# Edge sums of a graph network: sixteen edge tiles share one stretch of PSUM columns, with columns read as 5-bit steps

## The reference

```python
h = jnp.maximum(_layernorm(x), 0.0)
agg_src  = segment_sum(h[src], dst, 6250)
agg_edge = segment_sum(edge_attr_128, dst, 6250)
x = x + relu(concatenate([h, agg_src, agg_edge], 1) @ W.T + b)

h = jnp.maximum(_layernorm(x), 0.0)
h = relu(mean_agg(h) @ W1_l + b1 + h @ W1_r)     # mean over h[src] of the edges into each node
x = x + relu(mean_agg(h) @ W2_l + b2 + h @ W2_r)
```

## Time and profile before

| | |
|---|---|
| device time, 3 runs | 2033.34 us median (2031.09 to 2033.35) |
| profiled execution | span 1450.0 us from the first to the last instruction; its own device time is not recorded |
| build stage | about 117 to 665 us of the span |
| busy share of the span | PE 94%, PEld 85%, DVE 56%, POOL 45%, ACT 34% |

### The profile page before, as it was taken

One profiled execution on the slowest core, in us unless ns is written; L12 is line 12 of the kernel. 1 busy time (PEld: TensorE's weight loads), 2 busy tenths in 40 slices (PEclk: granted clock), 3 DMA queues, 4 the chain that ended last, 5 costly groups with the idle time before them and its releaser, 6 DMA issues.

```text
span 1450.0 us, 34753 instructions
## 1 busy us (share of the span) xinstructions
PE 1368.8 (94%) x12165; PEld 1235.0 (85%) x12166; DVE 812.4 (56%) x1837; ACT 490.1 (34%) x1389; POOL 654.9 (45%) x772
## 2 busy tenths in 40 slices
PE   3777999999999999998999999999999999999996
PEld 3656999999999899997888888888888888888885
DVE  8686898888888888882454545432222222221221
ACT  2632123455688888882333232311111110000000
POOL 5400000011121121215777777167777745777775
PEclk9988999999999999999999999999999999999998
DMA  6108778888999988886565556566666665666663
GB/s 182 29 2 221 202 221 230 242 248 237 261 271 266 273 260 260 262 269 222 161 214 177 175 199 162 193 195 196 205 196 207 187 194 190 220 210 214 213 203 74
DMA packets 284762, 295.12 MB, mean 204 GB/s; under 512 B 19461, under 2 KB 250064, under 8 KB 284672
## 3 DMA queue, kind: packets, MB, share of 16 engines
q1 hardware_dynamic: 233861, 212.90, 46.9%
q0 software_dynamic: 26016, 69.24, 16.9%
q10 hardware_dynamic: 24795, 11.74, 2.8%
HBM read 245.70 MB, written 48.11 MB: 203 GB/s over the span
## 4 chain that ended last, share of the span: by engine, by line
PE 84%; POOL 2%; issue 2%; DMA 2%; ACT 2%; DVE 0%; ACTq 0%; POOLq 0%; DVEq 0%; SPq 0%
PE edge_banks L1065 41%; PE edge_banks L1023 20%; PE banks L997 10%; PE edge_banks L1096 4%; PE edge_banks L1019 4%; PE banks L1083 3%; POOL shared L833 2%; ACT shared L1252 1%; DMA shared<-in_edge_attr 1%; PE edge_banks L1072 1%; PE banks L1077 1%; ACT banks L1247 0%; DMA shared<-g_rows,list_src 0%; DMA shared<-counts 0%; ACT shared L1229 0%
## 5 line engine op out<-in xcount | busy, mean ns | idle before, releaser
L833 POOL DMA_INDIRECT shared<-g_rows,list_src x555 | 541.9, 976 | 230.8 <-issue 167.2
L1065 PE MATMUL edge_banks<-g_even,shared 128*128 128x257 f16 (+1 forms) x3822 | 444.7, 273 | 4.4 <-DMA shared<-counts 4.4
L1065 PEld LDWEIGHTS edge_banks<-g_even,shared 128*128 128x128 fp8e3 x3822 | 372.4, 97 | 62.6 <-issue 4.6
L1023 PE MATMUL edge_banks<-shared 128*128 128x128 f32 x2744 | 345.3, 277 | 4.4 <-issue 4.0
L1023 PEld LDWEIGHTS edge_banks<-shared 128*128 128x128 f32 x2744 | 325.8, 193 | 7.6 <-issue 7.0
L812 POOL DMA_DIRECT2D counts<-shared x156 | 76.4, 490 | 487.8 <-ACT shared L1252 472.8
L1639 DVE SCALAR_TENSOR_TENSOR shared<-edge_banks,shared,own 128x128 f32<-128x128 f32 x98 | 34.3, 350 | 367.6 <-PE edge_banks L1065 339.4
L1065 PE MATMUL edge_banks<-shared 128*128 128x256 f16 x1911 | 225.8, 272 | 0.2 <-DVE own L1621 0.2
L1551 DVE TENSOR_TENSOR shared<-iota,shared 128x3528 f16<-128x3528 f16 x98 | 195.5, 1995 | 51.2 <-PE banks L997 50.8
L1252 ACT ACTIVATE shared<-banks 128x392 uint16<-128x392 f32 x312 | 152.2, 488 | 184.6 <-PE banks L997 174.2
L1065 PEld LDWEIGHTS edge_banks<-shared 128*128 128x128 fp8e3 x1911 | 185.3, 97 | 30.7 <-DVE own L1621 0.5
(11 more groups left out here) (278 smaller groups left out, 997.6 us busy)
## 6 DMA issues: line engine op xcount, KB each, us to landing
shared<-in_edge_attr SPq DMA_DIRECT2D x195, 512.0 KB, 4.5
shared<-counts SPq DMA_DIRECT2D x117, 784.0 KB, 5.2
counts<-shared POOLq DMA_DIRECT2D x156, 196.0 KB, 3.8
shared<-g_rows,list_src POOLq DMA_INDIRECT x555
shared<-hot_rows SPq DMA_DIRECT2D x20, 304.0 KB, 2.9
g_rows<-g_even SPq DMA_DIRECT2D x1, 3136.0 KB, 15.5
g_rows<-shared ACTq DMA_DIRECT2D x49, 64.0 KB
g_rows<-g_even ACTq DMA_DIRECT2D x49, 64.0 KB
```

The lines of the kernel that those rows point to most:

```text
L833: pool.indirect_dma_start(ring_g[use % RING][:, t, 0:2 * D], None, g_rows[r], bass.IndirectOffsetOnAxis(ap=list_src[:, at:at + 1], axis=0) ...
L1023: mm = pe.matmul(edge_wide[bank][:, :, at], ring[:, bank * GROUP_TILES + j, :], hot_dst[u][:, k, (j - 1) * SPREAD:j * SPREAD].unsqueeze(1) ...
L1065: mm = pe.matmul(acc[s][:, 0:wide], stream8[slot][:, order[h], :], G[r % 2][:, order[h], 0:wide], start=h == 0, stop=h == BLOCKS - 1, skip ...
```

## The change

The two groups of an iteration now share one stretch of 170 columns in one bank, so that there is one clearing product of 170 columns per iteration instead of two of 128, and one addition of 170 columns into `edge_t` instead of two of 128. The one-hots are 24 columns wide instead of 32, and written three times instead of four (3 x 170 = 510 of the bank's 512 columns). Offsets are counted from the start of the iteration's stretch. A group's four offsets no longer fit into three fields of 128; they are packed as one start and three steps of 5 bits, so the sequencer shifts, masks and adds them up. For k=1 all four offsets are needed, for k=0 three. DVE waits once, not twice, for `edge_free` in an iteration, and in a loop's pass a wait for `hot_ready` stands ahead of `hot_a`; the numbers that PE waits for on `edge_free` are halved.

```diff
-REACH = 32
-SPREAD = 32
-COPIES = 4
-EDGE_COLS = 128
-COL_UNIT = 128
+REACH = 24
+SPREAD = 24
+COPIES = 3
+EDGE_COLS = 170
+STEP_BITS = 5
...
-        edge_ps = [flat[i][:, 0:EDGE_COLS] for i in range(4)]
-        edge_wide = [f.rearrange("p (k c) -> p k c", c=EDGE_COLS) for f in flat]
+        edge_ps = [flat[i][:, 0:EDGE_COLS] for i in range(2)]
+        edge_wide = [flat[i][:, 0:COPIES * EDGE_COLS].rearrange("p (k c) -> p k c", c=EDGE_COLS) for i in range(2)]
...
                                     if n == HALF - 1:
-                                        pe.wait_ge(S["edge_free"], i * 2 + 3)
+                                        pe.wait_ge(S["edge_free"], i + 2)
...
                         def edges(k, packed, load_next):
-                            bank = 2 * u + k
-                            low, middle, high, rest = col_regs[u][k]
-                            pe.reg_alu(rest, packed, COL_UNIT, ALU.python_divide)
-                            pe.reg_alu(low, rest, -COL_UNIT, ALU.mult)
-                            pe.reg_alu(low, low, packed, ALU.add)
-                            pe.reg_alu(high, rest, COL_UNIT, ALU.python_divide)
-                            pe.reg_alu(middle, high, -COL_UNIT, ALU.mult)
-                            pe.reg_alu(middle, middle, rest, ALU.add)
-                            col = [0] + [pe.snap(g, donate=True, min_val=0, max_val=EDGE_COLS - SPREAD) for g in (low, middle, high)]
-                            for c in col[1:]:
-                                pe.lower_val((c + bank * 512) * 4 + (PSUM_BASE + BANKS * 2048) if bank else c * 4 + (PSUM_BASE + BANKS * 2048))
-                            pe.wait_ge(batch_landed[bank], it * 16 + 16)
-                            pe.matmul(edge_ps[bank], ring[:, bank * GROUP_TILES, :], hot_dst[u][:, k, FIRST_HOT:GROUP_HOT],
-                                      start=True, stop=True, skip_group_check=True)
-                            for j in range(1, GROUP_TILES):
-                                at = slice(0, SPREAD) if j < PAIR else bass.ds(col[j // PAIR], SPREAD)
-                                mm = pe.matmul(edge_wide[bank][:, :, at], ring[:, bank * GROUP_TILES + j, :],
-                                               hot_dst[u][:, k, (j - 1) * SPREAD:j * SPREAD].unsqueeze(1).broadcast_to([P, COPIES, SPREAD]),
+                            batch = 2 * u + k
+                            col = col_regs[u][k]
+                            step = step_regs[u][k]
+                            pe.reg_alu(col[0], packed, 3 * STEP_BITS, ALU.logical_shift_right)
+                            for q in range(1, 4):
+                                pe.reg_alu(step, packed, (3 - q) * STEP_BITS, ALU.logical_shift_right)
+                                pe.reg_alu(step, step, (1 << STEP_BITS) - 1, ALU.bitwise_and)
+                                pe.reg_alu(col[q], col[q - 1], step, ALU.add)
+                            moved = [pe.snap(g, donate=True, min_val=0, max_val=EDGE_COLS - SPREAD) for g in col]
+                            for c in moved[1 - k:]:
+                                pe.lower_val((c + u * 512) * 4 + (PSUM_BASE + BANKS * 2048) if u else c * 4 + (PSUM_BASE + BANKS * 2048))
+                            pe.wait_ge(batch_landed[batch], it * 16 + 16)
+                            for j in range(GROUP_TILES):
+                                tile = ring[:, batch * GROUP_TILES + j, :]
+                                if k == 0 and j == 0:
+                                    pe.matmul(edge_ps[u], tile, hot_dst[u][:, FIRST_HOT:WINDOW_HOT], start=True, stop=True, skip_group_check=True)
+                                    continue
+                                at = slice(0, SPREAD) if k == 0 and j < PAIR else bass.ds(moved[j // PAIR], SPREAD)
+                                n = k * GROUP_TILES + j - 1
+                                mm = pe.matmul(edge_wide[u][:, :, at], tile,
+                                               hot_dst[u][:, n * SPREAD:(n + 1) * SPREAD].unsqueeze(1).broadcast_to([P, COPIES, SPREAD]),
                                                start=False, stop=True, skip_group_check=True)
...
                     dve.tensor_tensor(hot_b, iota_b, along(b_tab, LO_B), ALU.is_equal).then_inc(S["b_ready"], 1)
+                    if not first:
+                        dve.wait_ge(S["hot_ready"], it * 2)
                     dve.tensor_tensor(hot_a, iota_a, along(a_tab, LO_A), ALU.is_equal)
...
-                        for k in range(2):
-                            dve.wait_ge(S["edge_free"], i * 2 + (k + 1))
-                            add_edges(bass.ds(at[2 * u + k], EDGE_COLS), 2 * u + k)
+                        dve.wait_ge(S["edge_free"], i + 1)
+                        add_edges(bass.ds(at[u], EDGE_COLS), u)
```

More of the change, by code:

```diff
@@ L169, in message_passing @@
         hot_bv = place(6264, LO_B * STEPS_ROW // 2).bitcast(F16).rearrange("p (l s) -> p l s", s=STEPS_ROW)
-        GROUP_HOT = GROUP_TILES * SPREAD + EDGE_COLS - SPREAD
-        FIRST_HOT = (GROUP_TILES - 1) * SPREAD
-        hot_dst = [place(6408 + i * 2 * GROUP_HOT, 2 * GROUP_HOT).rearrange("p (k c) -> p k c", c=GROUP_HOT) for i in range(2)]
-        assert 6408 + 4 * GROUP_HOT <= 8500
+        WINDOW_HOT = TILES_IT * SPREAD + EDGE_COLS - SPREAD
+        FIRST_HOT = (TILES_IT - 1) * SPREAD
+        hot_dst = [place(6408 + i * WINDOW_HOT, WINDOW_HOT) for i in range(2)]
+        assert 6408 + 2 * WINDOW_HOT <= 8500 and COPIES * EDGE_COLS <= 512 and REACH <= 1 << STEP_BITS
         ring = place(8500, 4096).rearrange("p (j c) -> p j c", c=D)
@@ L982, in build @@
                 col_regs = [[registers(pe, 4, f"col{u}_{k}_") for k in range(2)] for u in range(2)]
+                step_regs = [registers(pe, 2, f"step{u}_") for u in range(2)]
                 pe.wait_ge(S["words_taken"], WORDS)
@@ L1383, in _ @@
             dve.tensor_scalar(in_dense, w8_i[0:HOLDERS, 0:PER], float(DENSE * WINB), None, ALU.is_lt)
-            link(dve.tensor_scalar(col_pack, ident[:, 3 * PAIR::GROUP_TILES], float(COL_UNIT), None, ALU.mult))
-            link(dve.tensor_tensor(col_pack, col_pack, ident[:, 2 * PAIR::GROUP_TILES], ALU.add))
-            link(dve.tensor_scalar(col_pack, col_pack, float(COL_UNIT), None, ALU.mult))
-            dve.tensor_tensor(col_pack, col_pack, ident[:, PAIR::GROUP_TILES], ALU.add)
+            of_pair = [ident[:, q * PAIR::GROUP_TILES] for q in range(4)]
+            unit = float(1 << STEP_BITS)
+            link(dve.scalar_tensor_tensor(out=col_pack, in0=of_pair[0], scalar=unit, in1=of_pair[1], op0=ALU.mult, op1=ALU.add))
+            link(dve.scalar_tensor_tensor(out=col_pack, in0=col_pack, scalar=unit, in1=of_pair[2], op0=ALU.mult, op1=ALU.add))
+            dve.scalar_tensor_tensor(out=col_pack, in0=col_pack, scalar=unit - 1.0, in1=of_pair[3], op0=ALU.mult, op1=ALU.add)
             dve.wait_ge(S["base_up"], 2)
@@ L1531, in build, with add_edges @@
                 dve.wait_ge(S["zeroed"], 2 * BANKS)
-                def add_edges(at, bank):
-                    dve.tensor_tensor(edge_t[:, at], edge_t[:, at], edge_ps[bank], ALU.add).then_inc(S["edge_free"], 1)
+                def add_edges(at, u):
+                    dve.tensor_tensor(edge_t[:, at], edge_t[:, at], edge_ps[u], ALU.add).then_inc(S["edge_free"], 1)
                 def body(it, first):
@@ L1573, in build @@
                     body(it, False)
-                last = registers(dve, 4, "last_base")
-                dve.load(last, bases[:, NGROUP:NGROUP + 4])
-                for k in range(4):
-                    dve.wait_ge(S["group_done"], NGROUP + 1 + k)
-                    dve.wait_ge(S["edge_free"], NGROUP + 1 + k)
-                    add_edges(bass.ds(dve.snap(last[k], donate=True, min_val=0, max_val=NPAD), EDGE_COLS), k)
-                dve.wait_ge(S["edge_free"], NGROUP + 5)
+                last = registers(dve, 2, "last_base")
+                dve.load(last, bases[:, ITERS:ITERS + 2])
+                for u in range(2):
+                    dve.wait_ge(S["group_done"], NGROUP + 2 + 2 * u)
+                    dve.wait_ge(S["edge_free"], ITERS + 1 + u)
+                    add_edges(bass.ds(dve.snap(last[u], donate=True, min_val=0, max_val=NPAD), EDGE_COLS), u)
+                dve.wait_ge(S["edge_free"], ITERS + 3)
                 dve.sem_inc(S["edges_ready"], 2)
```

34 lines of the change are left out of this document (17 added, 17 removed).

## The result

The changed kernel takes 2095.28 us (median of 4 runs, 2093.06 to 2103.28) against 2033.27 us for the kernel before: a ratio of 1.0319, with a 95% interval of 1.0298 to 1.0339. It is 62.0 us slower. 2103 us had been predicted, with a range of 2070 to 2132. The profiled execution took 2095.03 us, with a span of 2093.3 us.

A forecast was written before the change was run, and what follows sets the result against it. PE was taken to bound the build stage, its sequencer 9% behind and bounding after the change: 12.45 against 10.99 us per pass, 1.46 over 48 passes, 70 us added to 2033.3, giving 2103 us, range 2070 to 2132.

The forecast's parts named there:

- What bounds: Build stage: PE bounds at 10.3 us per pass, its sequencer is second at 9.4 and needs 11.9 after the change.
- The offsets, 1.14 us per group: Sequencer ahead of each group: nine instructions take 0.60 us plus nine steps of 0.06, against 0.52 us before.
- The second rival: Sequencer's offset decoding: divisions are cheap by these divisors, 11.6 us per pass with slow loads, +29 us, 2062; chance 5%.
- The pass with short loads, 11.9 us: Sequencer's loop pass in the build stage: 9.4 us plus 2.5 for the new offsets, with register loads at their median.
- Slow loads, 0.55 us: Sequencer's register loads: those slower than the median add 0.55 us per pass, making 12.45 us.
- The sum: Build stage: 12.45 - 10.99 = 1.46 us per pass, over 48 passes 70 us, giving 2103 us.
- Columns worth nothing: PE's edge products: 72 columns instead of 128 gain nothing, since the weight load sets the pace at 0.111 us each.
- DVE worth nothing: DVE in the build stage: an iteration falls from 5.1 to 4.7 us, but DVE only waits longer for PE; no gain.
- The clock: PE's clock in the build stage: full speed expected; as fourth rival it falls, 2142 if one pass in ten is hit; 6%.
- PE's slices still show nines: Sign in the new trace's build stage: holes in PE, which would no longer be busy at nine tenths.
- The last stage: Sign in the new trace, after the build stage: this stage would be as long as before.
- the reading of 583.3 us: Whole program: device time was taken to lie 583.3 us above the profiled span, 1450 before and 1520 after.

## Why the prediction was right

- **What bounds.** Right: PE's sequencer was the second bound and became the first; its pauses for the queue went from 46 to one. Twenty added sequencer instructions per pass give 61 us in the kernel before, and repacked decoding gives 51 of 67 us back in the changed one.
- **The offsets, 1.14 us per group.** About 1.03 measured: 0.49 in instructions, nine steps of 0.06. The mis-sized term is the division, priced at 0.08. L1011 holds two and takes 0.083 to 0.088, not 0.18. The second rival had the direction right and its effect too large (0.85 us per pass; all decoding instructions together came out 0.44 cheaper).
- **The pass with short loads, 11.9 us.** 11.74 to 11.78 measured (the shortest passes). The cheaper divisions are in part made up by the distance between instructions: 66 instructions, 7.05 us recorded in them, and 4.7 us between them, 0.071 each, where the added ones had been given 0.06.
- **Slow loads, 0.55 us.** 12.29 - 11.76 = 0.53. The mean of 192 loads is 0.99 us, against 1.06 before: thinner traffic helps a little, as allowed for.
- **The sum.** +70 us predicted, +62 measured: of the 8 us between them, the pass with short loads is nearly all. That its two errors (divisions too dear, distances too short) pull against each other is luck. So is that the profile of before, from another chip, gave 10.99 and not the 10.87 of its repeat, from which the same sum would have been 6 us larger.
- **Columns worth nothing.** Right: 0.11 us apart at 72 as at 128 columns. The wider clearing product costs about the 0.12 us per pass that was estimated: 0.13 where PE sets the pace, in the kernel with packed decoding.
- **DVE worth nothing.** Right: an iteration's one-hot takes 0.55 us (0.52 estimated) and its addition 0.32 (0.33), and DVE waits 170 us for the count steps.
- **The clock.** Right at 1.00 for this kernel. The reason given, the 196 columns of the 36 count steps, was not enough by itself: they are all there with one copy too, and the clock was 0.50. The whole build stage at that clock takes 19.3 us per pass, not 20.6.
- **Misses.** PE's slices still show nines: 91% busy is enough for one. The last stage was not as long as before, and the reading of 583.3 us was wrong; both concern the chip and don't enter the sum.
- The loss in microseconds hardly depends on the chip (62 and 67), but its percentage does: 3.2% on the one kind of chip, 4.6% on the other.

The two rows of DVE, 220 to 400 us, that answer to the earlier trace rows:

```profile
L1572 DVE TENSOR_TENSOR shared<-iota,shared 128x384 f32<-128x384 f16 x30 | 16.5, 551 | 0.0
L1539 DVE TENSOR_TENSOR edge_t<-edge_t,edge_banks 128x170 f32 x29 | 9.4, 323 | 0.0
```

## What to carry to other kernels

Count the sequencer as an engine: in a loop with register arithmetic, add up its recorded durations, plus the distance between instructions, and set the sum against the pass; it shows in no busy share. When data are packed more tightly, look at what the unpacking compiles to, since the number of instructions costs more than the operations in them. And look at the longest stretch in which the sequencer issues nothing to PE: merging the loads was to save 0.6 us of its time in a pass and made the pass 0.3 to 1.0 us longer even at full clock, because the stretch around the branch became longer than a full queue could bridge.

## What the runs showed of the hardware

- **Between two register instructions** of PE's sequencer pass 58 to 63 ns in which nothing is recorded, as much as or more than the single operations themselves (32 to 43 ns). The Trainium skill (Perfetto Trace Analysis, Sequencer-only Instruction) says that a profile shows only the execution of such an instruction and not what lies around it; the rows agree.
- **Packed operations** run at very different rates: two divisions (L1011) in 83 to 88 ns, six plain ones in 74 to 79 (L1003 and L1017), but the seven of L1009 in 230. Multiplying by a positive number and subtracting made it 253, so the sign of its multiplier isn't the reason; what is stays open.
- **Register loads** go by the number of registers: about 0.86 us for 12 and 1.66 for 24.
- **PE's queue**: each time the sequencer had stood still for over 0.3 us ahead of the branch, 17 matmuls and 16 weight loads had not begun, in the kernel before (38 passes of its repeat) as with one copy at half clock (49 passes), and no pass of any run shows more there. The Trainium skill (TensorE: Matmul & The Clock Gate, Architectural detail: the array is 16× 32×32, not 1× 128×128) gives the queue a depth of 64. These runs show 33 instructions, so the measured figure decides here.
- **The clock**: with 24 columns per edge product the granted clock was 0.50 (1.2 GHz) over 920 us in all of which PE was busy; with 72 it was 1.00 (2.4 GHz) in the changed kernel, with PE busy for 91% of the time, but 0.50 for 54 us of the loop when its decoding was packed and its loads were merged.
- **The last stage** of the same program took about 785 us on some chips and about 1350 on others, with PE waiting on "issue".
